# A third bank for the turned feature chunks of a linear-attention stage

## The reference, cut to what matters

```python
q = (hidden_states @ Wq.T).reshape(b, t, HEADS, FEAT).transpose(0, 2, 1, 3)
k = (hidden_states @ Wk.T).reshape(b, t, HEADS, FEAT).transpose(0, 2, 1, 3)
v = (hidden_states @ Wv.T).reshape(b, t, HEADS, HD).transpose(0, 2, 1, 3)
mu = x.mean(axis=-1, keepdims=True)              # of q and of k, over the 16 features of a head
var = ((x - mu) ** 2).mean(axis=-1, keepdims=True)
xn = (x - mu) / jnp.sqrt(var + LN_EPS) * gamma + beta
```

## Time and profile before

| what | value |
| --- | --- |
| median of 3 runs | 2800.76 us (2800.25 to 2806.41) |
| the profiled execution | 2800.65 us, its span 2798.9 us |
| features_pass within the span | from about 1683 to 1949 us |
| busy over the whole span | PE 88%, DVE 79%, ACT 63%, POOL 20% |
| granted TensorE clock over the span | 0.957 of full speed |
| bytes moved over the span | 309.46 MB, 111 GB/s |

### The profile page before, as it was taken

One profiled execution on the slowest core, in us unless ns is written; L12 is line 12 of the kernel. 1 busy time (PEld: TensorE's weight loads), 2 busy tenths in 40 slices (PEclk: granted clock), 3 DMA queues, 4 the chain that ended last, 5 costly groups with the idle time before them and its releaser, 6 DMA issues. The chain is left out here.

```text
span 2798.9 us, 57238 instructions
## 1 busy us (share of the span) xinstructions
PE 2453.4 (88%) x15239; PEld 1154.6 (41%) x15239; DVE 2199.1 (79%) x5740; ACT 1770.1 (63%) x2700; POOL 562.9 (20%) x644
## 2 busy tenths in 40 slices
PE   5888999999999999568999997994999999996756
PEld 3442333333333333255666665653233333333545
DVE  6887999999999998286777767996666676666968
ACT  2452666666666666317777756884778788873546
POOL 1543212121111111240000000222222222222300
PEclk9996999999999999899999998997999999998979
DMA  6985353535353533350000002556867776664503
GB/s 186 287 281 119 78 111 76 113 76 111 78 109 79 106 83 83 98 169 1 0 0 0 0 0 76 180 187 180 161 143 143 150 140 145 142 139 116 148 9 118
DMA packets 224106, 309.46 MB, mean 111 GB/s; under 512 B 32416, under 2 KB 170352, under 8 KB 211952
## 3 DMA queue, kind: packets, MB, share of 16 engines
q1 hardware_dynamic: 223616, 307.47, 45.7%
q10 hardware_dynamic: 432, 1.31, 0.2%
HBM read 181.29 MB, written 126.88 MB: 110 GB/s over the span
## 5 line engine op out<-in xcount | busy, mean ns | idle before, releaser
L947 ACT ACTIVATE a_p<-psum 128x1024 f32<-128x1024 f32 (+1 forms) x640 | 567.0, 941 | 303.3 <-PE psum L1045 303.1
L947 ACT ACTIVATE b_p<-psum 128x512 f32<-128x512 f32 (+2 forms) x640 | 444.2, 749 | 146.0 <-PE psum L1045 142.9
L999 DVE CUSTOM_DVE_ANT_0 a_dump<-psum,a_bias 128x128 bf16<-128x128 f32 (+3 forms) x1024 | 446.2, 488 | 56.1 <-PE psum L1034 48.4
L997 DVE TENSOR_REDUCE a_peak<-psum 128x1 f32<-128x512 f32 x512 | 334.7, 688 | 27.8 <-PE psum L1034 25.2
L976 DVE COPY b_twin<-psum 128x512 f32<-128x512 f32 (+1 forms) x320 | 204.0, 637 | 165.6 <-PE psum L1045 162.3
L1045 PE MATMUL psum<-b_qs,b_ks 96*128 96x512 bf16 (+3 forms) x1536 | 307.1, 330 | 29.6 <-DMA b_vs<-values 29.6
L1061 PE MATMUL psum<-b_p,b_vs 128*32 128x512 f32 (+3 forms) x3072 | 314.7, 497 | 6.4 <-POOL b_p L919 6.4
L919 POOL TENSOR_SCALAR_AFFINE_SELECT a_p<-a_p 128x512 f32<-128x512 f32 x256 | 163.0, 637 | 752.4 <-ACT a_p L947 740.9
L1034 PE MATMUL psum<-a_ks,a_qs 96*128 96x128 bf16 (+2 forms) x1008 | 277.3, 333 | 19.0 <-DVE a_peak L999 14.0
L919 POOL TENSOR_SCALAR_AFFINE_SELECT b_p<-b_p 128x512 f32<-128x512 f32 x256 | 160.0, 637 | 441.6 <-DVE b_p L979 430.3
L1045 PE MATMUL psum<-a_qs,a_ks 98*128 98x512 bf16 x1008 | 233.9, 327 | 13.1 <-DMA a_qs<-a_rows 10.9
(11 more groups left out here) (197 smaller groups left out, 3648.2 us busy)
## 6 DMA issues: line engine op xcount, KB each, us to landing
qk_parts<-l_parts SPq DMA_DIRECT2D x96, 256.0 KB, 3.2
qk_parts<-g_parts SPq DMA_DIRECT2D x96, 256.0 KB, 3.1
values<-l_vx SPq DMA_DIRECT2D x64, 256.0 KB, 3.4
sums<-a_osb SPq DMA_DIRECT2D x64, 256.0 KB, 2.1
m_num<-sums SPq DMA_DIRECT2D x64, 256.0 KB, 3.7
m_inv<-reciprocals SPq DMA_DIRECT2D x64, 256.0 KB, 4.5
values<-g_vx SPq DMA_DIRECT2D x64, 256.0 KB, 2.9
sums<-b_osb SPq DMA_DIRECT2D x64, 256.0 KB, 3.2
```

Source lines behind the costliest of these rows:

```text
L947: act.activation(p[s % SLOTS][:, 2 * k:2 * k + heads, cols], m.psum[:, at:at + heads, cols], ACT.Exp if softmax else ACT.Square, scale=z.D ...
L997: last = dve.tensor_reduce(dst, piece, AX.X, ALU.max)
L999: last = dve.tensor_tensor_reduce(dump[c % SRING][:, at:at + w], piece, bias[:, 512 - w:], 1.0, NEG, ALU.add, ALU.max, dst)
```

## The change

The four chunks of a group get banks 5, 6, 7 and again 5. Chunk j now waits for `4 * n + max(j, 2)`: the chunks 0, 1 and 2 wait for all evictions of the group before, and chunk 3 also for the eviction of chunk 0 of its own group, since they share bank 5.

```diff
-        T0, Q0, VB, F0 = 0, 2, 4, 5
+        T0, Q0, VB = 0, 2, 4
+        feature_bank = [m.bank[j] for j in (5, 6, 7, 5)]
...
-                    act.activation(feat[u][:, j, :], m.bank[F0 + j % 2], ACT.Identity, bias=m.beta_col[:, 0:1],
+                    act.activation(feat[u][:, j, :], feature_bank[j], ACT.Identity, bias=m.beta_col[:, 0:1],
                                    scale=m.gamma_col[:, 0:1]).then_inc(feat_ready, 1)
...
-                    pe.wait_ge(feat_ready, 4 * n + j + 1)
+                    pe.wait_ge(feat_ready, 4 * n + max(j, 2))
                     for t in range(G):
-                        last = pe.transpose(m.bank[F0 + j % 2][:, t * P:(t + 1) * P], qk[u][:, t, j * P:(j + 1) * P],
+                        last = pe.transpose(feature_bank[j][:, t * P:(t + 1) * P], qk[u][:, t, j * P:(j + 1) * P],
                                             m.ident[:, :])
```

## The result

The changed kernel takes 2793.57 us (median of 7 runs, 2791.39 to 2794.65) against 2800.76 us: a ratio of 0.9973, with a 95% interval of 0.9964 to 0.9982. Its profiled execution took 2794.65 us with a span of 2792.9 us. Two more measurements beside the experiments gave 0.9973 (0.9962 to 0.9983) and 0.9975 (0.9965 to 0.9984).

What follows compares the result with a forecast made beforehand. A closed ring of PE and ACT, 14.45 us a group, was taken as the bound, with DVE held by POOL next at 14.09. 4.6 + 0.9 + 1.34 = 6.8 us less gave 2793.9 us, range 2791.0 to 2798.3.

Steps and rivals of the forecast that it cites:

- The ring of PE and ACT: Steady groups: PE's turns, projection and ACT's evictions form a closed ring, going from 14.45 to 13.78 us.
- POOL's hold of DVE as the next bound: Steady groups: DVE's scaling L1641 cannot finish its first piece before POOL's end plus 0.55, giving a period of 14.09 us.
- The end of the stage: Behind the last steady scaling the ring of PE and ACT sets the end again: 0.9 us of lead plus 1.34.
- the lead: PE and ACT run ahead of DVE in steady groups until L1707 waits for the fourth L1627: 0.9 us.
- The last group: DVE's cast may start ahead of POOL: between nothing and 1.1 us gained, taken as nothing.
- The sum: Over the stage: 4.6 + 0.9 + 1.34 = 6.8 us saved.
- the steady gain: Eleven steady L1641 from 1740.19 to 1884.66 gain 0.355 us each, 3.9 us.
- Rival B: Steady groups: DVE let go only at POOL's end, gaining 0.23 us a group; 5.4 us in all, 2795.4; chance 0.16.
- Rival C: DVE not held in steady groups, so fourteen groups gain the whole 0.67 us: 9.4 us, 2791.4; chance 0.08.
- D: Nothing comes of it: DVE's wait only moves elsewhere or POOL's hold costs the gain; time stays at 2800.8; chance 0.09.
- E: Slower through a lower granted clock while PE waits for DVE; some 10 us per group at that level; chance 0.07.

Runs made afterwards that it cites:

- e1: Changed kernel with its three banks, but each chunk waits for the eviction it waited for before: 2799.68 us, ratio 0.9995.
- e2: Changed kernel with POOL's third part of the split computed for two of four chunks only: 2784.26 us, ratio 0.9943.
- e4: Changed kernel with one more POOL subtraction per group, a quarter of the size, ahead of L1666: 2808.86 us, ratio 1.0027.
- e7: Changed kernel with DVE normalising ahead of scaling the heads and ACT evicting features ahead of taking the turned input: 2791.08 us, ratio 0.9966.
- e5: Changed kernel with DVE normalising a new group ahead of scaling the heads: 2793.79 us, ratio 0.9979.

## Why the prediction was right

- **The ring of PE and ACT, 0.67 us a group.** Right: e1 shows that the waits are all of the change, and e2 that the ring without the second wait is 13.78 us. The first group, before POOL's work begins, went from 14.37 to 13.69 us.
- **POOL's hold of DVE as the next bound.** Right in kind, and e2 to e4 show it as the cause. The price was 0.06 us a group too high: a period of 14.03, not 14.09. From the start of the third L1628 to the start of the cast behind the fourth it is now 1.18 us (1844.26 to 1845.44), where it was 1.25 (1845.23 to 1846.48). The fourth had been released by ACT's squares at just that time, which no row called a wait. That made 5.2 us up to the end of the last steady scaling, not 4.6. The same small gaps were in DVE's own work, put at 13.78 us; e7 makes it some 13.63.
- **The end of the stage.** 2.4 us more came from there up to the last scaling's end, not the 2.24 of 0.9 + 1.34. Part of the lead was too small: ACT's L1684 had been waiting for PE's turn by 0.15 us, and does so no longer.
- **The last group.** The cast did get ahead of POOL, and POOL was then held, as the Trainium skill (SBUF - State Buffer, "Who interferes with whom") has it: the one that starts first keeps the port. DVE gained 0.2 us, where I had taken nothing, with 1.1 as the upper bound. POOL's L1666 took 0.8 us longer, and DVE's L1652 waited 4.0 us for it, so most of what the early cast won was lost again.
- **The sum**: 6.8 forecast, 7.8 in the stage's trace, 7.2 in the medians. Step by step the terms that were off are the steady gain (3.9, measured 4.5), the end (2.2, measured 2.4) and the last group (0, measured 0.2). That the median, 2793.57, lies only 0.3 us from the forecast of 2793.9 is in part luck: single executions of this kernel spread over 3.3 us, and the stage gained 1.0 us more than forecast.
- **Rival B** (DVE let go only at POOL's end) is out: the held first pieces end 0.54 to 0.55 us behind it in all fourteen groups of the changed kernel's trace that have one, and in e4. **Rival C** is what e2 has, with POOL's work halved. **D** is out by the period. **E** is out too: the granted clock was 1.00 from 1732 to 1888.
- The span alone, 6.0 us shorter, would have told of a gain below the forecast, where the stage's 7.8 is above it; the difference is the late start of that execution.

## What to carry to other kernels

A wait on a closed ring is worth its length only down to the next ring, and a ring may run through an engine that waits for nobody: here DVE's scaling was held by POOL's use of what they share, and the trace of before showed it in this stage only in the last groups. Before moving work forward, look for what it will start to overlap. And two orders that bring little alone (here 0.04 us a group for DVE's, nothing for ACT's) can make 0.33 us together, when each shortens one of two rings. An instruction that has only been seen behind the other engine's end has not been shown to be free of it: L177 at its usual 1.38 us in e5 looked so, and e7 moved it 0.3 us into POOL's time.

## What the runs showed of the hardware

- DVE's scaling (two inputs in SBUF) and its cast stand still while POOL's subtraction runs (a first piece of 3.89 us for 0.68, a cast of 5.12 for 1.22 in the trace of before), and POOL stands still while DVE's cast runs: started 0.27 us behind the cast, POOL's L1666 ended 3.92 us behind the cast's end, against 4.05 us when alone.
- A held first piece of the scaling ends 0.54 to 0.55 us behind POOL's end though it takes 0.68 us when free; a delay of about 115 ns behind the other's end, as the Trainium skill (SBUF - State Buffer, "A bandwidth-pool intuition that's wrong") reports for descriptors, is not seen here.
- L177 (one input in SBUF, two scalars per partition) is held as well: its piece ends 0.15 us behind POOL's end, eleven times in e7 (469 to 489 ns for some 410), and in the first pass of before (2591 ns beside a memset, 982 and 1241 ns beside a subtraction). It ends sooner behind POOL than the scaling does, and no run shows why.
- DVE's statistics (L156, L160), sums of squares (L1628) and reciprocal L171 run beside POOL without such a hold: in e7 no piece of L156 takes over 0.41 us, of L160 over 0.18, of L1628 over 0.69 or of L171 over 0.17, the longest that they take without POOL being 0.42, 0.18, 0.69 and 0.18.
- The stage repeats to the hundredth of a microsecond in three traces of the changed kernel (234.54 us), while single executions of one kernel differ by several microseconds, all of them ahead of this stretch or behind it. For a change within one stage, its length in the trace tells more than the whole time.
